# Value biases written into PSUM by ScalarE ahead of TensorE, and value low parts taken by VectorE, in a two-network graph kernel

## What is computed

```python
u = jnp.einsum('bid,bjd->bij', h, h) / temper
a = jax.nn.softmax(u, axis=-1)
delta = a * adjacency_matrix
attn = delta / (jnp.sum(delta, axis=-1, keepdims=True) + 1e-10)
hl = h @ wl.T + b_l
hs = h @ ws.T + b_s
hr = h @ wr.T + b_r
ctx = attn_upper @ hl + diag(attn) * hs + attn_lower @ hr
o = (ctx - mean) / jnp.sqrt(var + LN_EPS) * g + beta
h = relu(o)
```

## Time and profile before

| what | value |
|---|---|
| median of 3 runs | 1750.47 us (1748.83 to 1750.87) |
| the profiled execution | 1750.89 us, of which the span of its instructions is 1749.1 us |
| TensorE busy, matmuls | 1694.3 us of the span |
| VectorE, ScalarE, GpSimd busy | 1253.8, 883.8, 824.5 us |
| mean granted TensorE clock | 0.993 of full speed |

### The profile page before, as it was taken

How to read it: one execution, slowest core, us unless ns; L and a number is a source line. 1 busy time by engine, 2 the same in 40 slices (tenths; PEclk the granted TensorE clock), 3 DMA queues, 4 the chain that set the end, 5 groups by cost and what they waited for, 6 DMA issues and landing times.

```text
span 1749.1 us, 30427 instructions
## 1 busy us (share of the span) xinstructions
PE 1694.3 (97%) x9856; PEld 1597.7 (91%) x9856; DVE 1253.8 (72%) x2735; ACT 883.8 (51%) x1785; POOL 824.5 (47%) x860
## 2 busy tenths in 40 slices
PE   7999999999999999999999999999999999999994
PEld 6989989888988989988899999999999999999994
DVE  4587685958768586776867767677676776766766
ACT  4545455464554646455454545545445454554542
POOL 5143242424324243334556747567375664656635
PEclk9999999999999999999999999999999999999997
DMA  7014021020301202030120210202102011020200
GB/s 225 1 31 154 6 85 35 24 90 10 110 6 37 82 25 90 6 114 18 63 76 19 69 46 22 93 0 72 43 21 93 0 65 50 21 94 0 76 1 36
DMA packets 76384, 92.20 MB, mean 53 GB/s; under 512 B 29600, under 2 KB 67488, under 8 KB 76320
## 3 DMA queue, kind: packets, MB, share of 16 engines
q1 hardware_dynamic: 76320, 91.51, 15.9%
HBM read 53.75 MB, written 25.17 MB: 45 GB/s over the span
## 4 chain that ended last, share of the span: by engine, by line
PE 40%; issue 35%; POOL 13%; DVE 8%; ACT 3%; SPq 1%; DMA 0%; POOLq 0%; DVEq 0%; ACTq 0%
PE b_work L1143 25%; PE b_work L1155 5%; POOL g_qv_lo L621 3%; POOL b_ht L601 3%; PE b_work L355 2%; PE b_turn L1104 2%; PE b_score_ps L105 2%; DVE b_z L1515 1%; DVE b_z L1472 1%; POOL s_v_lo L1330 1%; PE b_score_ps L369 1%; PE b_work L379 1%; POOL g_keep_l L616 1%; POOL g_sigma L630 1%; POOL g_a_nat L617 1%
## 5 line engine op out<-in xcount | busy, mean ns | idle before, releaser
L1143 PE MATMUL b_work<-b_w_hi,b_ht 128*128 128x384 f32 x2304 | 615.4, 339 | 4.5 <-DVE s_v_full L1438 4.5
L1143 PEld LDWEIGHTS b_work<-b_w_hi,b_ht 128*128 128x128 f32 x2304 | 419.3, 188 | 6.5 <-DVE s_v_full L1438 6.4
L1143 PE MATMUL b_work<-b_w_lo,b_ht 128*128 128x384 f32 x1152 | 386.0, 335 | 0.0
L355 PE MATMUL b_work<-b_ht,b_w_hi 128*128 128x512 f32 x1152 | 358.3, 392 | 9.9 <-DVE b_w_lo L696 9.9
L1330 POOL TENSOR_TENSOR s_v_lo<-s_v_full,s_v_hi 128x384 fp32r<-128x384 f32 x256 | 247.0, 982 | 186.8 <-ACT s_v_hi L1238 186.0
L621 POOL TENSOR_TENSOR g_qv_lo<-g_v_full,g_qv_hi 128x384 fp32r<-128x384 f32 x128 | 132.7, 1056 | 362.0 <-ACT g_qv_hi L494 362.0
L355 PEld LDWEIGHTS b_work<-b_ht,b_w_hi 128*128 128x128 f32 x1152 | 216.5, 189 | 51.7 <-issue 9.9
L355 PE MATMUL b_work<-b_ht,b_w_lo 128*128 128x512 f32 x576 | 226.1, 393 | 0.0
L1143 PEld LDWEIGHTS b_work<-b_w_lo,b_ht 128*128 128x128 f32 x1152 | 217.3, 189 | 0.0
L719 DVE TENSOR_TENSOR g_qv_lo<-b_work,g_qv_hi 128x512 fp32r<-128x512 f32 x192 | 128.7, 686 | 112.4 <-ACT g_qv_hi L482 110.6
L379 PE MATMUL b_work<-b_w_hi,b_ht 128*128 128x384 f32 x768 | 206.6, 336 | 0.0
(11 more groups left out here) (138 smaller groups left out, 3219.1 us busy)
## 6 DMA issues: line engine op xcount, KB each, us to landing
b_x_in<-in_x_t SPq DMA_DIRECT2D x16, 768.0 KB, 6.9
g_x_res<-in_x SPq DMA_DIRECT2D x16, 768.0 KB, 7.7
x<-b_z SPq DMA_DIRECT2D x16, 768.0 KB, 3.8
b_x_in<-x SPq DMA_DIRECT2D x16, 768.0 KB, 5.1
s_x_res<-b_x_in SPq DMA_DIRECT2D x16, 768.0 KB, 5.9
out<-b_z SPq DMA_DIRECT2D x15, 768.0 KB, 3.6
b_a_tr<-in_adj_t SPq DMA_DIRECT2D x64, 64.0 KB, 3.4
g_a_nat<-in_adj SPq DMA_DIRECT2D x32, 64.0 KB, 2.4
```

What stands on the lines that cost most here:

```text
L355: mm = pe.matmul(bank[:], w, h, start=(n == 0), stop=(n == len(pairs) - 1))
L1143: mm = pe.matmul(bank[:, 0:H], h, w, start=(n == 0), stop=(n == len(pairs) - 1))
```

## The change

It concerns the second network only. For sides 0 and 1 ScalarE copies the bias into the PSUM bank before TensorE's matmuls (`seed`), and these are issued with `start=False`, so that they add to it. ScalarE then reads the sum from the bank and rounds it to `v_hi` (`value_hi`), and VectorE subtracts `v_hi` from the bank to get `v_lo`, which is what frees the bank. Side 2 stays as it was. `v_full` and GpSimd's `values_lo` go. The orders of the ScalarE, GpSimd and VectorE programs are rewritten to match: ScalarE has eight seeds in a unit, the first two ahead of its exponentials; GpSimd does its four `gain_and_shift` together and then `diagonal`; VectorE takes `probabilities` before jobs 3 to 5, and `probabilities_lo` before job 6.

```diff
@@ -1136,18 +1134,23 @@
...
                     pe.wait_ge(split, side + 1)
-                bank = work_bank(i, unit, j)
+                if side < 2:
+                    pe.wait_ge(seeded, nth(i, unit, 2 * NT, 2 * t + side))
+                    bank = work[(unit * WN + j) % RING]
+                else:
+                    bank = work_bank(i, unit, j)
...
                 for n, (h, w) in enumerate(pairs):
-                    mm = pe.matmul(bank[:, 0:H], h, w, start=(n == 0), stop=(n == len(pairs) - 1))
+                    mm = pe.matmul(bank[:, 0:H], h, w, start=(n == 0 and side == 2), stop=(n == len(pairs) - 1),
+                                   skip_group_check=True)
...
                 for t in range(NT):
-                    pe.wait_ge(v_lo_ready, nth(i, unit, 2 * NT, 2 * t + 1))
+                    pe.wait_ge(work_free, freed(i, unit, t * SIDES + 1))
@@ -1232,11 +1235,18 @@
...
 
-            def values_hi(i, unit, t):
-                for n in range(2):
-                    act.wait_ge(work_free, freed(i, unit, t * SIDES + n))
-                    nc.scalar.activation(v_hi[:, t, n, 0:H], v_full[:, (2 * t + n) % VF, :], ACT.Copy)\
-                        .then_inc(v_hi_ready, 1)
+            def seed(i, unit, j):
+
+                t, side = value_job(j)
+                act.wait_ge(work_free, freed(i, unit, j - RING))
+                nc.scalar.activation(work[(unit * WN + j) % RING][:, 0:H], bias[:, side, layer_of(unit), :], ACT.Copy)\
+                    .then_inc(seeded, 1)
+
+            def value_hi(i, unit, j):
+                t, side = value_job(j)
+                act.wait_ge(work_full, nth(i, unit, WN, j))
+                nc.scalar.activation(v_hi[:, t, side, 0:H], work[(unit * WN + j) % RING][:, 0:H], ACT.Copy)\
+                    .then_inc(v_hi_ready, 1)
@@ -1253,19 +1263,31 @@
...
             def first_half(i, unit):
+                seed(i, unit, 0)
+                seed(i, unit, 1)
                 exponentials(i, unit)
-                values_hi(i, unit, 0)
+                seed(i, unit, 3)
+                value_hi(i, unit, 0)
+                value_hi(i, unit, 1)
+                seed(i, unit, 4)
+                seed(i, unit, 6)
...
             def second_half(i, unit, more, tail):
-                values_hi(i, unit, 1)
+                value_hi(i, unit, 3)
+                value_hi(i, unit, 4)
+                seed(i, unit, 7)
...
                     gated_normalise(1)
-                values_hi(i, unit, 2)
+                value_hi(i, unit, 6)
+                seed(i, unit, 9)
+                value_hi(i, unit, 7)
+                seed(i, unit, 10)
...
                         turn_out(i, unit + 1, k)
-                values_hi(i, unit, 3)
+                value_hi(i, unit, 9)
+                value_hi(i, unit, 10)
@@ -1287,16 +1309,28 @@
...
             gated_contexts_out()
+            seed(0, 0, 0)
+            seed(0, 0, 1)
             exponentials(0, 0)
+            seed(0, 0, 3)
             probabilities_hi(0, 0)
+            value_hi(0, 0, 0)
+            value_hi(0, 0, 1)
+            seed(0, 0, 4)
+            seed(0, 0, 6)
             gated_normalise(0)
-            for t in range(3):
-                values_hi(0, 0, t)
-                if t == 1:
-                    weight_hi(0)
+            value_hi(0, 0, 3)
+            value_hi(0, 0, 4)
+            seed(0, 0, 7)
+            weight_hi(0)
+            value_hi(0, 0, 6)
+            seed(0, 0, 9)
+            value_hi(0, 0, 7)
+            seed(0, 0, 10)
...
                 turn_out(0, 1, k)
-            values_hi(0, 0, 3)
+            value_hi(0, 0, 9)
+            value_hi(0, 0, 10)
@@ -1323,12 +1357,6 @@
...
                 op.then_inc(keep_ready[s], 1)
-
-            def values_lo(i, unit, t):
-                for n in range(2):
-                    pool.wait_ge(v_hi_ready, nth(i, unit, 2 * NT, 2 * t + n))
-                    nc.gpsimd.tensor_tensor(v_lo[:, t, n, 0:H], v_full[:, (2 * t + n) % VF, :],
-                                            v_hi[:, t, n, 0:H].bitcast(F32), ALU.subtract).then_inc(v_lo_ready, 1)
@@ -1361,22 +1389,13 @@
...
                     roots(i, unit)
-                    if more:
-                        values_lo(i, unit + 1, 0)
...
                     if layer == 1:
-                        for t in range(NT // 2 if more else LAST_GT):
+                        for t in range(NT if more else LAST_GT):
...
                     if more:
-                        values_lo(i, unit + 1, 1)
                         diagonal(i, unit + 1)
-                    if layer == 1 and more:
-                        for t in range(NT // 2, NT):
-                            gain_and_shift(i, s, t)
-                    if more:
-                        values_lo(i, unit + 1, 2)
-                        values_lo(i, unit + 1, 3)
@@ -1390,17 +1409,11 @@
...
             pool.wait_ge(sh.next_small, 16 * 7)
-            nc.gpsimd.memset(v_hi[:, :, :, H:HC].bitcast(F32), 1.0)
-            nc.gpsimd.memset(v_lo[:, :, :, H:HC].bitcast(F32), 0.0)
...
             pool.wait_ge(power_set, 1)
-            values_lo(0, 0, 0)
-            values_lo(0, 0, 1)
             diagonal(0, 0)
+            masks(0, 1, first=True)
             weight_lo(0)
-            values_lo(0, 0, 2)
-            masks(0, 1, first=True)
-            values_lo(0, 0, 3)
@@ -1427,16 +1440,15 @@
...
                 t, side = value_job(j)
-                dve.wait_ge(work_full, nth(i, unit, WN, j))
+                bank = work[(unit * WN + j) % RING]
                 if side < 2:
-                    if 2 * t >= VF:
-
-                        dve.wait_ge(v_lo_ready, nth(i, unit, 2 * NT, 2 * t + side - VF))
-                    dst = v_full[:, (2 * t + side) % VF, :]
+                    dve.wait_ge(v_hi_ready, nth(i, unit, 2 * NT, 2 * t + side))
+                    nc.vector.tensor_tensor(v_lo[:, t, side, 0:H], bank[:, 0:H], v_hi[:, t, side, 0:H].bitcast(F32),
+                                            ALU.subtract).then_inc(work_free, 1)
                 else:
-                    dst = v_own[:, t, 0:H]
-                nc.vector.tensor_tensor(dst, work[(unit * WN + j) % RING][:, 0:H], bias[:, side, layer, :],
-                                        ALU.add).then_inc(work_free, 1)
+                    dve.wait_ge(work_full, nth(i, unit, WN, j))
+                    nc.vector.tensor_tensor(v_own[:, t, 0:H], bank[:, 0:H], bias[:, side, layer, :], ALU.add)\
+                        .then_inc(work_free, 1)
@@ -1544,11 +1556,11 @@
...
                 more = not (last and unit == UNITS - 1)
+                probabilities(i, unit)
...
                     biased_value(i, unit, j)
-                probabilities(i, unit)
+                probabilities_lo(i, unit)
                 biased_value(i, unit, 6)
-                probabilities_lo(i, unit)
@@ -1608,6 +1620,8 @@
...
             nc.vector.memset(v_own[:, :, H:H + 1], 1.0)
+            nc.vector.memset(v_hi[:, :, :, H:HC].bitcast(F32), 1.0)
+            nc.vector.memset(v_lo[:, :, :, H:HC].bitcast(F32), 0.0)
```

More of the change, by code:

```diff
@@ L935, in softmax_layers @@
     LAST_GT = 1
-    VF = 4
     HALF = P // 2
@@ L956, in softmax_layers @@
         v_lo = sb("v_lo", [P, NT, 2, HC], F32R)
-        v_full = sb("v_full", [P, VF, H])
         v_own = sb("v_own", [P, NT, H + 1])
@@ L999, in softmax_layers @@
         diag_ready, own_ready = sem("diag_ready"), sem("own_ready")
-        v_hi_ready, v_lo_ready = sem("v_hi_ready"), sem("v_lo_ready")
+        v_hi_ready, seeded = sem("v_hi_ready"), sem("seeded")
         stats_ready, mean_ready, total_begun, total_ready, var_ready, rstd_ready, z_ready = (
```

## The result

The changed kernel takes 1862.07 us (median of 4 runs, 1859.41 to 1862.50), the kernel before takes 1750.54 us beside it: a ratio of 1.0639, with a 95% interval of 1.0626 to 1.0651. The prediction was 1862. The span of the profiled execution goes from 1749.1 to 1860.6 us, 111.5 us more, and the mean granted clock from 0.993 to 0.964.

A forecast was written before the change was run, and what follows sets the result against it. TensorE's queue was taken as the bound, its matmuls busy 861.0 of the second network's 877.2 us. Terms 94.2 - 6.4 - 7 + 23.8 + 3.2 + 4 = +111.8 us gave 1862 us, range 1832 to 1898.

The forecast's parts named there:

- heads of units 0 and 1: Job 0 waits for seed 0, queued behind `final_normalise`: 6.66 and 6.80 us later, in 7 passes, +94.2 us.
- waits for banks: TensorE's waits for banks not yet drained by VectorE, behind unit 1's head, vanish as TensorE comes later: -6.4 us.
- clock: TensorE's clock halves behind each of 14 waits at the heads, 1.7 us each: +23.8 us, bounds 0 and +42.
- `scores` in 16 units: In layer 1 a later `turn_lo` 2 makes `scores` 0.2 us late in 16 units: +3.2 us, bounds 0 and +10.
- first unit: Second network's first unit: first seed behind four copies, seeds 6 and 7 behind normalisation tiles; +4 us, bounds 0 and +12.
- rest of the units: ScalarE's new list inside a unit keeps up with TensorE: 0, bounds 0 and 1 us in each of 32 units.
- rival 1: The clock doesn't fall at the heads, so the wait alone remains: 1838 us; chance 0.12.
- rival 2: ScalarE falls behind inside the units, 1 to 2 us in each of 32: 1894 to 1926 us; chance 0.15.
- The walk through the list: ScalarE's layer 0 list, job by job: seed 7 ready at 9.8, wanted at 10.9, the tightest place.
- Rivals 3 and 4: Rival 3: heads cost less because VectorE catches up while TensorE waits, 1820 us, chance 0.07; Rival 4 has its own line.
- VectorE's way to `final_offset`: Faster residuals against a later job 10 bring unit 1's head forward 1.0 us: -7 us, bounds 0 and -14.
- Rival 4: Faster or no change: seeds of units 0 and 1 done in time, only existing waits go, 1738 us; chance 0.03.

The follow-up runs named there:

- wait_alone: Kernel before, plus only a wait: TensorE's first value job of units 0 and 1 waits for `final_normalise`; no seeds. 1851.71 us, ratio 1.0583.
- spread_final: Changed kernel with seeds 0 and 1 ahead of `final_normalise`, whose tiles are spread into the next unit, and rounding 9 ahead of the third turn. 1749.58 us, ratio 0.9997.
- before_edge_moved: Kernel before, with VectorE's loop body starting at the contexts of unit 1 instead of at unit 0, same order of work. 1744.77 us, ratio 0.9969.
- double_seeds: spread_final with each seed written twice, the second time once the first is done. 1800.26 us, ratio 1.0290.
- edge_moved: spread_final with VectorE's loop body starting at the contexts of unit 1, same instructions in the same order. 1768.76 us, ratio 1.0107.
- edge_elsewhere: spread_final with VectorE's loop cut between the row maxima and job 0 of unit 2, same instructions in the same order. 1738.35 us, ratio 0.9934.
- early_seeds: Changed kernel with seeds 0 and 1 of every unit moved behind the work of the unit before, ahead of `final_normalise`. 1820.88 us, ratio 1.0404.
- kept_busy_later: Changed kernel with 30 extra TensorE matmuls filling the wait at the heads of units 0 and 1, except in the first pass. 1833.46 us, ratio 1.0480.
- edge_moved_seed3: edge_moved with seed 3 ahead of the exponentials in ScalarE's list in layer 1 units. 1759.49 us, ratio 1.0060.

## Why the prediction was right, point by point

| step | predicted us | measured us |
|---|---|---|
| heads of units 0 and 1, with the wait for low parts at the end of unit 0 | +94.2 - 7.0 | 7 x (6.16 + 6.42) = 88.0, and 5.5 no longer waited: +82.5 |
| waits for banks | -6.4 | -5.6 |
| clock | +23.8 | +28.6 (by the trace 32.3) |
| `scores` in 16 units | +3.2 | +3.7 |
| first unit | +4 | +1.9 |
| rest of the units | 0 | 0 |
| sum | +111.8 | +111.1 (by the trace's clock 114.8), of 111.5 |

The mechanism is shown, but that the forecast met the median within 0.1 us is luck: the heads were 4.7 us too dear and the first unit 2.1, and the clock, 4.8 to 8.5 us too cheap, made up for them.

*Heads.* The mechanism is the one predicted, shown from both sides: the wait alone makes nearly all of the loss (wait_alone), and without it all of it goes (spread_final). The heads net came out at 82.5 against 87.2 us. VectorE reaches `final_offset` earlier than I had it: no residual is slow any more, with a longest of 557 ns where it was 1373, also at the end of unit 3, where I had put the gain as even (two of the four took 1.69 us there, at 1393.49). In the changed kernel no GpSimd operation runs beside a residual. The Trainium skill's rule on the shared ports (page "SBUF — State Buffer", section "SBUF: two separate sides") is borne out on this point: with GpSimd's low parts in the kernel the longest is 1371 ns (wait_alone), without them 557.

*Waits for banks.* They go because TensorE comes later, as forecast: in wait_alone they go too, with the stop at VectorE's loop edge still there (11.6 us in 5). Why they arose I had wrong. I put them down to VectorE being late with the contexts; before_edge_moved shows that they come from the stop at the loop edge, since they go when the edge is moved. The one in the first unit stays, so it is 5.6 us and not 6.4.

*Clock.* It falls behind each of the 14 waits, as forecast, and rival 1 is out. The term was too small: 2.0 us a time by the difference of the two kernels, 2.3 by the trace, in place of the 1.7 of the earlier trace rows; the upper bound of 3.0 held.

*Turns and `scores`.* 0.23 us in each of 16 units in place of 0.2; the weight loads wait 0.3.

*First unit.* Unit 1 starts at 881.97, before at 880.10. In this there are two things. TensorE waits 2.08 us for a seed of the first unit, and its clock does not fall behind that, where the wait of 2.04 us in the earlier trace rows did lower it and cost 1.7 us. Without this the change costs 3.6 us there, as wait_alone (878.33, clock not lowered) has it too.

*The rest of a unit.* Outside the first unit TensorE waits for no seed but those of the 14 heads, so rival 2 is out at a seed of 0.494 us. The walk through the list gave seed 7 a margin of 1.1 us. Measured, in a layer 0 unit, on ScalarE:

```profile
1518.50 0.50 ACT L1242 ACTIVATE b_work<-b_bias 128x384 f32<-128x384 f32 x1 [0.24 <-DVE s_v_lo L1446]
...
1520.23 0.49 ACT L1248 ACTIVATE s_v_hi<-b_work 128x384 fp32r<-128x384 f32 x1 [0.22 <-PE b_work L1145]
```

Seed 7 is done at 1519.0; rounding 6 had waited for the end of job 6 at 1520.23, so TensorE wanted the seed about 1520.05: 1.05 us. double_seeds bears out that this is the tightest place, since seed 7 is the only one that is late in every unit. It is not the only tight one: seed 0 and the third turn follow, and edge_moved shows that a late VectorE uses up seed 3's margin through the exponentials.

*Rivals 3 and 4.* The heads cost what they seemed to, since VectorE's way to `final_offset` is not shortened by TensorE's waiting. Rival 4's 1738 us needed "an order of ScalarE's list that the diff doesn't have". edge_elsewhere has such an order, with the loop edge moved besides, and takes 1738.35.

## What to carry to other kernels

When an operation is put ahead of the engine that sets the end, its place in its own engine's list comes first and its duration second (double_seeds, with twice the duration, costs 51 us; the wrong place cost 112): look for what that engine does at the moment when the first of them is wanted, and what that in turn waits for. Here 0.5 us of work behind a wait of 7 us cost 6.3 us each time, and the lowered clock behind it another 2.0. Moving the first two ahead took back only 41 of the 112 us; the next in the list must be walked too, and the loop edge of each engine counted as a stop of its own.

## What the runs showed of the hardware

*A stop at the loop edge of VectorE.* 2.3 us, 5 times, in the kernel before, the changed one and spread_final. The page's row of the queue that loads instructions (packets, MB, share of time), in the changed kernel:

```profile
q14 instruction: 43, 0.35, 0.1%
```

and in edge_elsewhere:

```profile
q14 instruction: 18, 0.15, 0.0%
```

Without the stop there are 18 or 19 packets, with it 43 or 44. edge_moved also has 43, with the cut that gave 19 in before_edge_moved, and the times of the packets show that it has the stop at every edge. Between 1110 and 1690 us, edge_elsewhere and before_edge_moved have no packet of this queue, and edge_moved has these:

```profile
q14 instruction: 25, 0.20, 0.1%
```

Two of them fall into each of VectorE's stops that I looked at, such as 1461 to 1467. What decides whether packets come at a loop's edge stays open.

*The clock near 2 us of waiting.* TensorE's waits of 3.07 us and more in the second network lowered the clock each time, in all profiles. Near 2 us both happen: 2.04 us in the kernel before did (and 2.08 in early_seeds and kept_busy_later), 2.08 in the changed kernel, 2.12 in wait_alone and even 2.60 in double_seeds did not. Waits of 0.9 to 1.5 us mostly didn't, but two close together, 1.35 and 0.84 us, did so once in edge_moved_seed3. In wait_alone:

```profile
866.90:870.00 3.10, 1.58 (x11) 1.61 (x12) 2.11 (x5) 2.05 (x5) 3.10 (x5) 1.00 0.17 25
870.00:872.40 2.40, 2.40 (x17) 2.40 (x16) 2.37 (x4) 0.09 (x1) 2.40 (x3) 1.00 0.57 214
```

That is the same wait as in the earlier trace rows, with a clock of 1.00 behind it where the earlier trace rows has 0.50. A single wait of this length can't be priced from one profile.
